# A graph layer's edge kernel: the paired groups permute their inputs as two float32r parts instead of their outputs in float32, and 12 of 28 pairs of groups are paired instead of 8 of 27

## What is computed

```
h    = relu(layernorm(x))
msg  = concat(h[dst[e]], edge_attr[e])              # for every edge e
hid  = relu(msg @ W1a.T + b1a)                      # 128 wide
sums = segment_sum(hid @ W1b.T + b1b, src)          # per node, by src
agg  = sums / max(counts, 1)
z    = relu(concat(h, agg) @ W2a.T + b2a) @ W2b.T + b2b
out  = x + concat(z, h) @ Wr.T + br
```

## Time and profile before

| | |
|---|---|
| median of 3 runs | 522.39 us (520.93 to 524.32) |
| profiled execution, span | 518.3 us |
| busy: PE, PEld | 431.0 us (83%), 390.0 us (75%) |
| busy: POOL, DVE, ACT | 356.1 us (69%), 298.0 us (57%), 285.0 us (55%) |
| scatters (L568, L551) | 300 and 64 |
| mean granted TensorE clock | 0.906 of full speed |
| DMA | 123.45 MB, mean 238 GB/s |

### The profile page before, as it was taken

One profiled execution on the slowest core, in us unless ns is written; L12 is line 12 of the kernel. 1 busy time (PEld: TensorE's weight loads), 2 busy tenths in 40 slices (PEclk: granted clock), 3 DMA queues, 4 the chain that ended last, 5 costly groups with the idle time before them and its releaser, 6 DMA issues.

```text
span 518.3 us, 9203 instructions
## 1 busy us (share of the span) xinstructions
PE 431.0 (83%) x3133; PEld 390.0 (75%) x3133; DVE 298.0 (57%) x825; ACT 285.0 (55%) x576; POOL 356.1 (69%) x406
## 2 busy tenths in 40 slices
PE   6655988899999999998689779845999787987795
PEld 4555777888796988878578778845998777987674
DVE  7868642534656657555425547414765537667884
ACT  3442957774787777786658378171633772100073
POOL 4777777777677777777777777777777777776000
PEclk9876696987999899988899889986999897999999
DMA  7998998553959477978553989996999997778631
GB/s 182 306 338 229 257 266 271 155 156 108 303 143 294 141 257 265 257 255 263 164 151 92 336 249 333 312 331 196 360 326 336 328 322 221 248 214 256 177 86 43
DMA packets 62319, 123.45 MB, mean 238 GB/s; under 512 B 9369, under 2 KB 33374, under 8 KB 62270
## 3 DMA queue, kind: packets, MB, share of 16 engines
q1 hardware_dynamic: 49598, 91.25, 59.0%
q0 software_dynamic: 12672, 31.58, 18.8%
HBM read 71.53 MB, written 51.25 MB: 237 GB/s over the span
## 4 chain that ended last, share of the span: by engine, by line
POOL 32%; PE 26%; DMA 13%; issue 13%; DVE 7%; ACT 5%; SPq 2%; POOLq 0%; ACTq 0%; DVEq 0%
POOL slots_dram L568 24%; PE bank L1261 10%; POOL pairs_dram L551 8%; DMA slots_dram<-pay,pos_i 7%; PE bank L1241 4%; PE bank L1270 4%; DMA dstb<-in_dst 4%; DVE oh L774 2%; DMA rows<-slots_dram 2%; ACT eo L1059 2%; SPq L475 1%; PE bank L1294 1%; PE bank L1291 1%; PE bank L1211 1%; PE bank L1362 1%
## 5 line engine op out<-in xcount | busy, mean ns | idle before, releaser
L568 POOL DMA_INDIRECT slots_dram<-pay,pos_i x300 | 289.0, 963 | 98.7 <-issue 89.6
L1261 PE MATMUL bank<-rows,oh 128*125 128x130 f32 x1100 | 139.5, 287 | 40.3 <-DVE oh L774 40.1
L1261 PEld LDWEIGHTS bank<-rows,oh 128*125 128x125 f32 x1100 | 133.3, 198 | 44.6 <-issue 43.4
L1059 ACT ACTIVATE eo<-dstb,minus_lane 64x256 f32<-64x256 int32 x190 | 85.1, 494 | 94.5 <-DMA dstb<-in_dst 79.8
L1241 PE MATMUL bank<-pw,eo 128*128 128x128 f32 x856 | 119.9, 299 | 3.5 <-ACT pay L1042 2.3
L1241 PEld LDWEIGHTS bank<-pw,eo 128*128 128x128 f32 x856 | 113.3, 213 | 11.4 <-issue 8.0
L774 DVE TENSOR_TENSOR oh<-bank,rows 128x1500 f32<-128x1500 f32 (+5 forms) x67 | 81.8, 1223 | 17.6 <-DMA rows<-slots_dram 10.4
L1270 PE MATMUL bank<-hid,xch 116*128 116x131 f32 (+1 forms) x512 | 68.3, 294 | 14.6 <-DVE xch L724 8.6
L1270 PEld LDWEIGHTS bank<-hid,xch 116*128 116x128 f32 (+1 forms) x512 | 65.3, 205 | 16.9 <-issue 9.9
L551 POOL DMA_INDIRECT pairs_dram<-pay,pos_c x64 | 61.5, 960 | 22.3 <-issue 18.0
L1064 ACT ACTIVATE eo<-eo,one 64x512 f32<-64x512 f32 x95 | 68.3, 719 | 3.1
(11 more groups left out here) (198 smaller groups left out, 376.7 us busy)
## 6 DMA issues: line engine op xcount, KB each, us to landing
rows<-slots_dram SPq DMA_DIRECT2D x24, 864.0 KB
dstb<-in_dst SPq DMA_DIRECT2D x54, 256.0 KB, 7.7
eo<-in_edges_T SPq DMA_DIRECT2D x54, 256.0 KB, 4.9
rows<-pairs_dram SPq DMA_DIRECT2D x12, 864.0 KB
...
slots_dram<-pay,pos_i POOLq DMA_INDIRECT x300
...
```

The costliest lines, as they stand in the source:

```text
L568: pool.indirect_dma_start(out=slots_dram[:, :], out_offset=bass.IndirectOffsetOnAxis(ap=pos_i[:, u, k:k + 1], axis=0), in_=pay[:, u, k, :] ...
L1059: last = A.activation(eo[p, g % EB, a * HB:(a + 1) * HB], dstb[p, g % DB // 2, a * HB:(a + 1) * HB], ACT.Square, bias=minus_lane[p, g // 2 ...
L1261: last = T.matmul(o[0:BN, v * SW:(v + 1) * SW], oh2[:, r % 2, n, :], rows[:, sum_no[r] % RR, n, 0:SW], start=(t == 0), stop=(t == TB[ph] - ...
```

## The change

The plan grows to 28 pairs, of which 12 are C and 16 are O (before: 27, 8 and 19). The C pairs' slots are kept in three regions. Phases of O pairs are 5, 5, 2, 2, 2 pairs, in place of 5, 5, 5, 2, 1, 1.

A C group is made in another order: first its inputs are permuted, then the hidden rows are made in permuted order. The features of an edge (62 one-hot columns of `dst`, its mark, its slot number, 64 edge features) stand in rows, split in a rounded part `x_hi` and a remainder `x_lo`, both of type float32r. For each unit four float32r matmuls (two parts by two tiles) with `perm` as the moving operand (256 columns) give the transposed, permuted features; ACT copies them to `moved`, and two float32 matmuls of 131 columns a unit (`paired_hidden`) give the hidden rows, mark and slot number at once; ACT's relu writes `pay2`. C groups no longer load `dst` broadcast over 64 partitions (256 KB) nor `edges_T` (256 KB), but one tile of rows (232 KB).

```diff
-ORDER = "OOOO" + "CO" * 8 + "O" * 7
+ORDER = "OOOO" + "CCO" * 4 + "CO" * 4 + "OOOO"
...
-    PAIRS = [5, 5, 5, 2, 1, 1]
+    PAIRS = [5, 5, 2, 2, 2]
+    PAIRED = [5, 5, 2]
...
-    C = [math.ceil((expected(ph) + 4 * math.sqrt(expected(ph))) / 128) for ph in range(NPH)]
+    C = [math.ceil((expected(ph) + 3.8 * math.sqrt(expected(ph))) / 128) for ph in range(NPH)]
...
-    AFTER_PHASE = [4, 4, 4, 2, 1, 0, 4]
+    AFTER_PHASE = [4, 4, 2, 2, 0, 4, 3, 2]
...
-    ROUNDS_FROM, FULL_FROM, EARLY_SHARE, SHARE, C_SHARE, MOST = 7, 10, 10, 23, -8, 32
+    ROUNDS_FROM, FULL_FROM, EARLY_SHARE, MOST = 7, 10, 10, 32
+    SHARES = dict(OO=25, CO=12, OC=14, CC=2)
...
-        units = [("perm", C_GROUPS.index(g - 1), u, 0) for u in range(UNITS)] if g - 1 in C_GROUPS else []
...
+        if g in C_GROUPS:
+            for half in range(2):
+                after[g].append(len(rounds))
+                rounds.append(("perm", C_GROUPS.index(g), half, 0))
...
+            def load_paired_edges(c):
+                if c >= XR:
+                    sp.wait_ge(S["xp"], c - XR + 1)
+                sp.dma_start(staged[:, c % XR].rearrange("p k f -> p (k f)"), edges_rows[c, 0:TILE_A, :]).then_inc(s_xe[c % XR], 16)
...
+            def features(c):
+                g, e, pair = C_GROUPS[c], ones_in(c), c // 2 % 2
+                lanes = slice(K * (c % 2), K * (c % 2) + K)
+                hi, lo = x_hi[:, c % XR], x_lo[:, c % XR]
+                dve.wait_ge(S["xhi"], c + 1)
+                dest = dest_x[0:TILE_A, pair, lanes]
+                V.tensor_copy(hi[:, :, e + SEEN], mark[0:TILE_A, g, :])
+                link(V.tensor_copy(hi[:, :, e + SEEN + 1], dest))
+                V.tensor_tensor(lo[:, :, e + SEEN + 1], dest, hi[:, :, e + SEEN + 1].bitcast(f32), ALU.subtract)
+                V.tensor_tensor(hi[:, :, e:e + SEEN], marks_all[0:TILE_A, e:e + SEEN].unsqueeze(1).to_broadcast((TILE_A, K, SEEN)),
+                                dst_x[0:TILE_A, pair, lanes].unsqueeze(2).to_broadcast((TILE_A, K, SEEN)), ALU.is_equal)
+                V.tensor_tensor(lo[:, :, edges_in(c)], staged[:, c % XR], hi[:, :, edges_in(c)].bitcast(f32), ALU.subtract).then_inc(S["xp"], 1)
...
-                for t in range(2):
-                    k = K * (c % 2) + 2 * u + t
-                    last = V.tensor_scalar(perm[:, n % PR, 256 * t:256 * t + 256], slot_no[0:TILE_A].rearrange("p h s -> p (h s)"),
-                                           slot_x[0:TILE_A, c // 2 % 2, k:k + 1], None, ALU.is_equal)
-                last.then_inc(S["ohp"], 1)
+                k = K * (c % 2) + 4 * half
+                V.tensor_tensor(perm[:, n % PR], slots_near[0:TILE_A].unsqueeze(1).to_broadcast((TILE_A, 4, 256)),
+                                slot_x[0:TILE_A, c // 2 % 2, k:k + 4].unsqueeze(2).to_broadcast((TILE_A, 4, 256)), ALU.is_equal).then_inc(S["ohp"], 1)
...
+            def round_features(c):
+                act.wait_ge(s_xe[c % XR], 16 * (c // XR + 1))
+                if c >= XR:
+                    act.wait_ge(S["ag"], last_perm[c - XR] + 1)
+                A.copy(x_hi[:, c % XR, :, edges_in(c)], staged[:, c % XR]).then_inc(S["xhi"], 1)
+
+            def copy_moved(r):
...
+                A.copy(moved[:, n % 2, :], bank[:, 4 + r % 2, :]).then_inc(S["ep"], 1)
...
+            def paired_hidden(c, half):
...
+                for u in (2 * half, 2 * half + 1):
...
+                    for side in range(2):
+                        first = 256 * (u % 2) + 128 * side
+                        last = T.matmul(bank[:, part % HIDDEN_BANKS, side * HW:(side + 1) * HW], moved[:, n % 2, first:first + 128], pwx[:, c % 2, u, :],
+                                        start=True, stop=True, skip_group_check=True)
...
-                    for side in range(2):
-                        for t, n in enumerate((TILE_A, TILE_B)):
-                            last = T.matmul(o[:, side * HW:(side + 1) * HW], perm[0:n, perm_no[r] % PR, 256 * t + 128 * side:256 * t + 128 * side + 128],
-                                            hid[0:n, c % HR, 2 * u + t, 0:HW], start=(t == 0), stop=(t == 1), skip_group_check=True)
+                    for u in range(2):
+                        for part in (x_hi, x_lo):
+                            for t, lanes in enumerate((TILE_A, TILE_B)):
+                                last = T.matmul(o[:, 256 * u:256 * u + 256], part[0:lanes, c % XR, 4 * half + 2 * u + t, :],
+                                                perm[0:lanes, n % PR, 2 * u + t, :], start=(part is x_hi and t == 0), stop=(part is x_lo and t == 1),
+                                                skip_group_check=True)
```

540 lines of the change are left out of this document (320 added, 220 removed).

## The result

The kernel after takes 582.08 us (median of 4 runs, 579.46 to 583.44) against 522.77 us for the kernel before beside it (4 runs, 520.93 to 524.32): ratio 1.115, 95% interval 1.108 to 1.122. Slower, by 59 us; forecast were 496 us, with a range of 484 to 520. The profiled execution's span is 577.5 us at a mean granted clock of 0.863 (before 518.3 and 0.906).

What follows compares the result with a forecast made beforehand. POOL's unbroken scatters were taken as the bound: their end at 478.0 less 32.9 gives 445.2, 6 us of starving makes 451, plus 40.3 to the end 491.5, plus 4.1 to the median 496 us; range 484 to 520.

Steps and rivals of the forecast that it cites:

- Scatters and their price: POOL's stream: 26 fewer scatters at an unchanged 1.2635 us each, 32.9 us off.
- Price of float32r: PE in a C group: 16 float32r matmuls of 256 columns at 0.115 us each, 1.84 us in all.
- rival (3): PE's float32r matmuls cost twice the price, 0.23 us: POOL starved for 35 us, 523 us, no change; chance 0.09.
- (4): PE's float32r matmuls run at the float32 rate, 0.46 us: about 605 us; chance 0.08.
- So PE needs its 188 us again, waits and cold clock included: PE, groups 8 to 32: work differs by -0.1 us, so PE reaches group 32 at 262.
- Averages over 24 groups: Groups 8 to 32: PE's and POOL's total work compared over the whole stretch, giving 6 us of POOL starved.
- the h and z rounds stay: PE, groups 8 to 32: these rounds were taken as unchanged, adding nothing to PE's difference.
- I cost all of these at nothing: DVE, ACT, load queues, DMA: their changes add no time, though DVE gets 1.4 us more a C group.
- as long as no wait is late: Condition on DVE's work, in all about 340 of 490 us, being hidden behind PE.
- no 2x is lost: DVE's one-hots: the old eight take 2.38 us, so the new ones lose no double-rate mode.
- Rival (2), latency in the runs: Waits in runs of four C groups cost 10 to 22 us beyond the forecast: 505 to 517 us; chance 0.15.
- After group 32 and the end: Groups 32 to 54: 184.5 us of POOL, no more starving; then 40.3 us to the end of the span.

Runs made afterwards that it cites:

- e11: Kernel after with its 12 C pairs never two in a row (OOOO, then twelve times CO), last paired region summed one group earlier: 561.72 us, ratio 1.072.
- e15: Kernel before with six of each C group's eight one-hots made twice on DVE: 529.57 us, ratio 1.017.
- e8: Kernel after without DVE's one-hots in x_hi and subtraction for x_lo from the third C group on: 564.81 us, ratio 1.078.
- e3: Kernel after with nearly all of ACT's one-hot work for the O groups left out: 554.75 us, ratio 1.068.
- e1: New C-group method with 8 C pairs in the order, phases and waits of before, but the shares of rounds of after: 543.73 us, ratio 1.047.

## Why the prediction was wrong

**Scatters and their price: right.** 338 scatters, 970 ns each and 1.26 us apart.

**Price of float32r: right.** 0.115 us was taken. In the timeline above two float32r matmuls begin 0.25 us apart (226.51, 226.76), 0.12 each; at the lower clock two take 0.43 (230.72 to 231.15), 0.21 each. As claims on the price at full clock, rivals (3) and (4) fall; where the clock is low, a C group does pay nearly the 0.23 of rival (3) (whose own sum slips: 35 for 6 us is 29 more, not 27).

**"So PE needs its 188 us again, waits and cold clock included": the step that failed.** It had PE at group 32 at 262 and gave the group to POOL at 267; PE came at 329.10 and POOL at 336.73, 70 us late. The sum of PE's work was nearly right: its difference to before was put at -0.1 us, and 200.1 us busy at a clock of 0.83 against 174.5 at 0.91 make, as an estimate, 166 us of work at full clock for 159. But it was laid on a span taken from another order, in which gaps were 13.5 of 188 us and the clock 0.91. With the new order PE is idle for 39.8 of 188 us and the clock is 0.81. In that window PE delivered 148.2 x 0.81 = 120 us of work at full clock; before it was 174.5 x 0.91 = 159.

**Averages over 24 groups: the mistake behind it, as far as the runs show.** I compared PE's and POOL's totals between groups 8 and 32. That holds if what one engine is ahead can be kept. But a C group gives POOL 5.05 us of work and an O group 10.1, and `pay` and `pay2` keep only a few groups: in a run of four C groups POOL uses up in 20 us what the chain makes in far more, and in the O groups behind it PE can't get ahead by more than the buffers hold. A block of four C and two O groups took 57 to 66 us (first scatters of groups 8, 14, 20, 26, 32: 96.21, 162.48, 221.00, 278.42, 336.73), where POOL needs 40.4. In e11 a block of two and two took 37.6, 37.1, 30.3, 32.7, 34.0 and 30.8 where POOL needs 30.3. On average a block with two more C groups took 26 us more, 13 each, where POOL's work for them is 5.05 each; the prediction had 47 us of PE for six groups. e11 shows this for the order, some 20 of the 59 us. For the 39 us that stay with no run of four, it is argued from the timelines, and the bunched z rounds stand beside it as a rival: the prediction said "the h and z rounds stay", but they moved together, most of them to groups 12 to 14.

**"I cost all of these at nothing" (DVE, ACT, queues): wrong.** The condition stood beside it, "as long as no wait is late", and was not tried on a single C group. DVE's work was also put too low: about 340 us, and 368.3 were measured. Nor does "no 2x is lost" follow from the 2.38 us of the old eight one-hots: an instruction of 4 columns takes 0.16 us here (L837), and eight times that is 1.3 us of them, which scaling one long instruction leaves out. In the kernel before DVE can hand over a unit's one-hots, a quarter of a group, after two instructions of 0.3 us. In the one after, five instructions of `features` and one of 1.21 us stand before PE's first matmul, and the ranks of the next pair between the two halves. e15 puts a price of 7 to 9 us (with an interval of 0 to 17) on 36 us of DVE's work, e8 17 on 23, e3 27 on 50 of ACT's.

**Rival (2), latency in the runs: right in kind, too small.** It had "1 us for each of 24 C groups, or 4 us for each of 8 runs", 505 to 517 us. Measured are 18 to 22 us of stalls in each of the four runs of four, 81.6 us together, where e11's C pairs apart have 4 us each; and 22 us in e1, in the old order. I had priced the waits one by one, not the chain of six hand-overs they form. `dst` was not the trouble: ACT's wait for it fell from 79.8 to 29.4 us.

**After group 32 and the end: a little short.** 192.0 us to the last scatter's start where 184.5 less one scatter was said, and 47.8 us behind the last scatter for 40.3. With the 70 us before group 32 this closes the sum: 491.5 + 69.7 + 8.8 + 7.5 = 577.5.

Not settled: how much of the 21 to 27 us that e1 loses in the old order is the halves' coarser hand-over, how much the bunched z rounds and how much the clock, and what sets the clock. Two versions weren't tried: one with the z rounds spread as before, and one with the hidden rows made one group later, which would take the chain off the path. No kernel that ran beats the one before.
